# Two-layer transformer kernel on one core: float32 products of the FFNs, the router and the second Q, K, V written as three float16 products each

## The chip, the core and the metric

The kernel runs on one core of a Trainium2 chip. A core has a matrix engine (PE, its weight loads are shown apart as PEld), a vector engine (DVE), a scalar engine (ACT), GpSimd (POOL) and a queue engine (SP) that here starts every DMA. The engines run on their own and wait for each other by semaphores. Matrix products land in PSUM, eight banks of 512 float32 columns for each of 128 partitions; POOL doesn't work on PSUM in this kernel. The metric is the time of one execution in device microseconds, and the figure of a kernel is the median of its runs. Lower is better.

## What is computed

```python
x = L0_attn_x                                   # (1, 2048, 256), float32
h = _layernorm(x) * (1 + ca) + sa               # shifts and scales from silu(c) @ wmod
x = x + ga * _L0_attn_ref(h, ...)               # 16 heads of 16, causal with a distance penalty
h = _layernorm(x) * (1 + cb) + sb
x = x + gb * _L0_ffn_ref(h, ...)                # silu(h @ gate.T * s) * (h @ up.T * s) @ down.T * s, 704 wide
h = _layernorm(x) * (1 + ca) + sa               # layer 1, with its own shifts, scales and gates
x = x + ga * _L1_attn_ref(h, ...)               # 16 heads of 16, every query sees every key
h = _layernorm(x) * (1 + cb) + sb
scores = sigmoid(h @ gate_w.T)                  # router: 8 experts, the best 2 of each token are used
x = x + gb * (shared_out + routed_out)          # experts of 176 and a shared part of 352: 1760 wide
```

## The kernel before

The 2048 tokens are worked on in four chunks of 512 (`tc` or `p` from 0 to 3). One Python list, the walk, holds all work in program order; each engine runs through it and takes its own share of each item, so the list sets the order on every engine. It has five stages:

0. Prologue: modulation, first layer norm, Q, K, V of layer 0.
1. Attention of layer 0. Each score block is made twice: once for the row maxima (`max` items, PE L722 and the DVE reduction L1156), and once transposed for the exponentials (PE L753, ACT L951), followed by the product with V (PE L778).
2. FFN 0 in six pieces of its hidden width (`hg` = gate product L818, `hid` = up product L826, then silu on ACT L990 and the product with it on DVE L1180), with the tail of attention 0 between its first pieces, and from the second token chunk on the down product `dn` (L847) of the chunk before, its add to x (DVE L1147), statistics `st`, normalisation `nm` (DVE L1099), transposition `ln` (PE L684, evicted by ACT L927 into hT), and `qk`, `v` (L695, L707) of layer 1. K and V parts go to DRAM and come back into the layout of attention (SP L506, L533, L521; `keys` and `rows` items). Early `max` blocks of attention 1 are strewn in.
3. Attention of layer 1.
4. Router and FFN 1 in 14 pieces, of which eleven are routed and have their hidden values multiplied by the token's weight of the expert (PE `we` L835, ACT L1000, DVE L1184 and L1187), and three are shared. The first six gate and up pairs go with the tail of attention 1.

Weights, features hT and hidden values are float32 in the products that the change touches. POOL has little to do: the reciprocal root of the variance (L609, L612) for each `st`, the scaling of w_o and x's bias (L618, L625) and the scaling of the down weights (L635), also in the walk's order. The products of stage 2 and 4 use four slots of two PSUM banks; `hg` with its `hid` alternates between two of them, and waits until what was there two uses ago is drained.

## Time and profile before

| | |
|---|---|
| median of 3 runs | 1790.18 us (1787.64 to 1791.87) |
| profiled execution, its own time | 1790.27 us |
| its span in the trace | 1788.5 us |
| mean granted TensorE clock | 0.952 |
| busy: PE, PEld | 1649.3 us, 698.8 us |
| busy: DVE, ACT, POOL | 1166.7, 1004.2, 61.7 us |

The span is the time from the first to the last instruction in the trace. Busy times of engines overlap, so they don't add up to it. The share of an engine over the whole span hides the stages: what a change in a stage is worth has to be read from that stage's own windows.

### The profile page before, as it was taken

What the parts mean: (1) busy time and instruction counts of PE and PEld (TensorE: products, weight loads), DVE (VectorE), ACT (ScalarE), POOL (GpSimd) and SP (SyncE); (2) the same over time, 40 slices, a digit from 0 to 9 for tenths busy, and PEclk for the clock granted to TensorE, in tenths of its full rate; (3) what the DMA queues carried; (4) which work ended last, traced back from release to release, by engine and by line L of the source; (5) the groups of instructions that cost most, each with busy time, mean ns of one, the idle gap of its engine ahead of it and who ended that gap; (6) DMA issues with size and microseconds to landing.
All of it is one profiled execution on the core that took longest, in us unless ns stands there. A gap on an engine that the chain in (4) does not pass through costs nothing.

```text
span 1788.5 us, 32558 instructions
## 1 busy us (share of the span) xinstructions
PE 1649.3 (92%) x12812; PEld 698.8 (39%) x12812; DVE 1166.7 (65%) x1438; ACT 1004.2 (56%) x1913; POOL 61.7 (3%) x96
## 2 busy tenths in 40 slices
PE   7878988898999999859999999999999999999998
PEld 5533333333324544412333323333232244646556
DVE  5567888988912256694798999899989414231221
ACT  2145667777884111008997988789878952121120
POOL 2100000001000000300000000000000020000000
PEclk8879999999999999868999999999999989999999
DMA  7610000000001210110200000000000010000000
GB/s 212 148 50 11 11 11 6 11 6 1 2 1 30 46 45 20 34 40 6 87 6 6 6 6 6 6 6 9 8 2 2 1 42 1 6 6 12 1 12 12
DMA packets 39542, 41.87 MB, mean 23 GB/s; under 512 B 7172, under 2 KB 37828, under 8 KB 39388
## 3 DMA queue, kind: packets, MB, share of 16 engines
q1 hardware_dynamic: 39396, 39.79, 8.5%
q8 instruction: 108, 1.77, 0.4%
q14 instruction: 38, 0.31, 0.1%
HBM read 29.02 MB, written 10.49 MB: 22 GB/s over the span
## 4 chain that ended last, share of the span: by engine, by line
PE 61%; DVE 26%; ACT 6%; issue 3%; SPq 2%; DMA 2%; DVEq 0%; ACTq 0%
DVE mpart L1156 22%; PE psum L778 14%; PE psum L753 9%; PE psum L847 8%; PE psum L818 8%; PE psum L826 7%; PE psum L722 6%; ACT probs L951 5%; PE psum L695 2%; PE psum L807 1%; PE psum L684 1%; DMA parts<-key_region 1%; DVE attn_region L1099 1%; PE psum L761 1%; PE psum L835 1%
## 5 line engine op out<-in xcount | busy, mean ns | idle before, releaser
L1156 DVE TENSOR_REDUCE mpart<-psum 128x2 f32<-128x1024 f32 (+2 forms) x832 | 915.8, 1158 | 116.6 <-PE psum L722 92.4
L951 ACT ACTIVATE probs<-psum 128x512 f32<-128x512 f32 (+3 forms) x1664 | 844.4, 573 | 192.7 <-PE psum L753 108.0
L778 PE MATMUL psum<-probs,v_region 128*17 128x256 f32 (+2 forms) x6144 | 497.6, 396 | 13.8 <-ACT out_sb L966 9.9
L722 PE MATMUL psum<-key_region,row_region 50*128 50x512 f16 (+3 forms) x1664 | 327.1, 385 | 75.2 <-DVE mpart L1156 72.9
L753 PE MATMUL psum<-row_region,key_region 52*128 52x512 f16 (+3 forms) x1664 | 356.9, 381 | 13.8 <-ACT probs L951 8.2
L753 PEld LDWEIGHTS psum<-row_region,key_region 52*128 52x128 f16 x1664 | 98.8, 93 | 372.8 <-ACT probs L951 279.2
L778 PEld LDWEIGHTS psum<-probs,v_region 128*17 128x17 f32 x6144 | 103.0, 95 | 208.0 <-issue 103.4
L722 PEld LDWEIGHTS psum<-key_region,row_region 50*128 50x128 f16 x1664 | 94.3, 94 | 182.6 <-DVE mpart L1156 128.6
L818 PE MATMUL psum<-hT,ffn_w 128*128 128x512 f32 (+1 forms) x320 | 157.4, 615 | 1.7 <-issue 0.9
L826 PE MATMUL psum<-hT,ffn_w 128*128 128x512 f32 (+1 forms) x320 | 153.2, 602 | 0.0
L990 ACT ACTIVATE probs<-psum 128x512 f32<-128x512 f32 (+1 forms) x56 | 33.4, 597 | 190.2 <-PE psum L818 190.2
L1184 DVE TENSOR_TENSOR probs<-psum,probs 128x512 f32<-128x512 f32 x44 | 30.4, 691 | 106.5 <-PE psum L826 106.5
L847 PE MATMUL psum<-v_region,key_region 128*128 128x256 f32 x448 | 97.5, 379 | 1.7 <-DVE key_region L1187 1.7
L1147 DVE TENSOR_TENSOR x_sb<-psum,x_sb 128x512 f32<-128x512 f32 x16 | 11.1, 692 | 127.0 <-PE psum L847 127.0
L847 PEld LDWEIGHTS psum<-v_region,key_region 128*128 128x128 f32 x448 | 85.0, 190 | 15.4 <-issue 3.9
L826 PEld LDWEIGHTS psum<-hT,ffn_w 128*128 128x128 f32 (+1 forms) x320 | 59.6, 189 | 77.2 <-issue 77.2
L818 PEld LDWEIGHTS psum<-hT,ffn_w 128*128 128x128 f32 (+1 forms) x320 | 56.1, 187 | 69.4 <-issue 66.4
L990 ACT ACTIVATE probs<-psum,gate_s 128x512 f32<-128x512 f32 (+1 forms) x24 | 16.5, 687 | 102.1 <-PE psum L818 102.1
L927 ACT ACTIVATE hT<-psum,modc 128x512 f32<-128x512 f32 x32 | 23.2, 775 | 78.4 <-PE psum L684 78.4
L1180 DVE SCALAR_TENSOR_TENSOR key_region<-psum,up_s,probs 128x512 f32<-128x512 f32 (+1 forms) x24 | 18.0, 749 | 65.7 <-PE psum L826 65.5
L1190 DVE TENSOR_TENSOR key_region<-psum,probs 128x512 f32<-128x512 f32 (+1 forms) x12 | 8.2, 690 | 67.8 <-PE psum L826 67.6
L958 ACT ACTIVATE mrow_t<-psum 128x512 f16<-128x512 f32 x32 | 19.1, 598 | 51.6 <-PE psum L735 51.0
(102 smaller groups left out, 930.1 us busy)
## 6 DMA issues: line engine op xcount, KB each, us to landing
parts<-key_region SPq DMA_DIRECT2D x32, 256.0 KB, 2.5
key_region<-parts SPq DMA_DIRECT2D x48, 128.0 KB, 4.3
row_region<-parts SPq DMA_DIRECT2D x192, 32.0 KB
key_region<-in_wmod SPq DMA_DIRECT2D x2, 1536.0 KB, 12.1
x_sb<-in_x SPq DMA_DIRECT2D x4, 512.0 KB, 8.3
row_region<-mrow_t SPq DMA_DIRECT2D x128, 2.0 KB
out<-x_sb SPq DMA_DIRECT2D x16, 128.0 KB, 1.8
ffn_w<-in_w_gate SPq DMA_DIRECT2D x1, 1760.0 KB, 7.2
```

The lines of the kernel that those rows point to most:

```text
L695: mm = pe.matmul(bank(b + f), w[:, k, f * P:(f + 1) * P], hT[:, k, tc * CH:(tc + 1) * CH], start=(k == 0), stop=(k == KD - 1))
L722: mm = pe.matmul(bank(b + par)[:, 0:w], rows[at, g, hp, r * P:(r + 1) * P], keys[at, g * HP + hp, q * CH:q * CH + w], start=True, stop=not ...
L753: mm = pe.matmul(bank((e + par) % 3)[:, off:CH], keys[at, g * HP + hp, jt * P:(jt + 1) * P], rows[at, g, hp, off:CH], start=True, stop=not ...
L778: mm = pe.matmul(psum[32 * h:32 * h + VW, SUM_BANK, lo:hi], v_sb[:, jt, g * HG + h, :], probs[:, (S0[y] + s) % 2, h, lo:hi], start=(jt == ...
L818: mm = pe.matmul(psum[0:f, b, :], up_gate[y][0][:, d, c * P:c * P + f], hT[:, d, tc * CH:(tc + 1) * CH], start=(d == 0), stop=(d == KD - 1))
L826: mm = pe.matmul(psum[0:f, b + 1, :], up_gate[y][1][:, d, c * P:c * P + f], hT[:, d, tc * CH:(tc + 1) * CH], start=(d == 0), stop=(d == KD ...
L847: mm = pe.matmul(bank(b)[:, r * D:(r + 1) * D], hid[y][tc % 2][0:f, c, (2 * z + r) * P:(2 * z + r + 1) * P], down[y][0:f, c, :], start=(c ...
L927: ins = nc.scalar.activation(hT[:, c, tc * CH:(tc + 1) * CH], bank(b + c), ACT.Identity, bias=modc[:, y, i:i + 1], scale=modc[:, y, i + 2: ...
L951: nc.scalar.activation(probs[:, (S0[y] + s) % 2, 2 * hp + par, off:CH], psum[:, e % 3, off:CH], ACT.Exp, scale=SCALES[y]).then_inc(s_p, 1)
L990: nc.scalar.activation(sil[k % 2][0:f, :], psum[0:f, bank_of(item), :], ACT.Silu, scale=gate_s[0:f, c:c + 1] if y == 0 else 1.0).then_inc( ...
L1156: V.tensor_reduce(mpart[:, n % NG, at:at + 2, q:q + 1], psum[:, b:b + 2, 0:w], AX.X, ALU.max).then_inc(drained(*item)[0], 1)
L1184: V.tensor_tensor(utmp[k % 2], up, sil[k % 2], ALU.mult).then_inc(s_ut, 1)
```

## The change

Each float32 operand of the products in question is held as two float16 numbers, high = float16(a) and low = float16(a - high), in the room of the float32 word. A product is then the sum of three float16 products in PSUM: high by high, high by low, low by high (`PRODUCTS`). This is done for gate, up and down of both FFNs, the router's logits, and Q, K, V of layer 1. Attention 0's Q, K, V, the output projections and attention itself stay as they are.

The halves are made on the chip. Weights arrive in float32 in the key region and POOL splits them (`split_projections`, `split_ffn`, `split_down`). A transposed and modulated feature block is written twice by ACT, in float32 to a temporary and in float16 to hT, and POOL subtracts (`low_features`). Hidden values go to a float32 temporary, ACT makes the high half (`high_hidden`), and the low one is subtracted on POOL in layer 0 and on DVE in layer 1 (`low_hidden`, item `hh`, one pair late). In FFN 0 the down products move from behind the first to behind the second pair, `nm`, `ln`, `qk` and `v` move later; in FFN 1 the down products move by one pair too.

```diff
+PRODUCTS = ((0, 0), (0, 1), (1, 0))
...
-            if c == 0:
+            if c == 1:
                 for it in down_halves(0, p):
                     out.append(it)
                     blocks(2 * many if tc > 2 else 0)
                 out.append(("st", 2, p))
-            if c == 1:
+            if c == 3:
                 out.append(("nm", 2, p))
-            if c == 2:
+            if c == 4:
                 out.append(("ln", 2, p))
                 blocks(many)
-            if c == 4:
+            if c == 5:
                 out.append(("qk", 1, p, 0))
                 blocks(many)
                 out.extend([("qk", 1, p, 1), ("keys", 1, p)])
                 blocks(many)
                 if p == 0:
                     out.extend([("rows", 1, n) for n in range(NG)])
-            if c == 5:
                 out.append(("v", 1, p))
...
-    out += flat(second[:1]) + down_halves(1, 0) + flat(second[1:])
+    out += flat(second[:2]) + down_halves(1, 0) + flat(second[2:])
...
+    out += [("load", 0), ("wp",), ("wf", 0), ("wd", 0)]
...
+def with_halves(items):
+
+    out, open_one = [], None
+    for it in items:
+        if it[0] == "dn" and it[3] == 0 and open_one and open_one[1:3] == it[1:3]:
+            out.append(("hh", *open_one[1:]))
+            open_one = None
+        out.append(it)
+        if it[0] == "hid":
+            if open_one:
+                out.append(("hh", *open_one[1:]))
+            open_one = it
+    return out
...
+            def split_ffn(y):
+                pool.wait_ge(s_wffn[y], 32)
...
+                for d in range(KD):
+                    for i in range(2):
+                        link(nc.gpsimd.tensor_copy(up_gate[y][i][:, 0, d, :], raw_up_gate[y][i][:, d, :]))
+                        ins = nc.gpsimd.tensor_tensor(up_gate[y][i][:, 1, d, :], raw_up_gate[y][i][:, d, :],
+                                                      up_gate[y][i][:, 0, d, :], ALU.subtract)
...
                 for c in range(NC[y]):
                     f = fsize(y, c)
-                    ins = nc.gpsimd.tensor_tensor(down[y][0:f, c, :], down[y][0:f, c, :], gab[0:f, y, D:2 * D], ALU.mult)
+                    link(nc.gpsimd.tensor_tensor(down_t[0:f, c % 2, :], raw_down[y][0:f, c, :], gab[0:f, y, D:2 * D], ALU.mult))
+                    link(nc.gpsimd.tensor_copy(down[y][c][0:f, 0, :], down_t[0:f, c % 2, :]))
+                    ins = nc.gpsimd.tensor_tensor(down[y][c][0:f, 1, :], down_t[0:f, c % 2, :], down[y][c][0:f, 0, :], ALU.subtract)
...
+            def low_features(item):
+                q, tc = item[1:]
+                pool.wait_ge(*drained(*item))
+                for c in range(KD):
+                    ins = nc.gpsimd.tensor_tensor(hT16[tc][:, 1, c, :], mod_t[xh_buf(q, tc)][:, c, :], hT16[tc][:, 0, c, :], ALU.subtract)
+                ins.then_inc(s_low, 1)
...
-                for d in range(KD):
-                    mm = pe.matmul(psum[0:f, b, :], up_gate[y][0][:, d, c * P:c * P + f], hT[:, d, tc * CH:(tc + 1) * CH],
-                                   start=(d == 0), stop=(d == KD - 1))
+                pe.wait_ge(s_f16, y + 1)
+                pe.wait_ge(*split_of(2 * y + 1, tc))
+                for m, (u, v) in enumerate(PRODUCTS):
+                    for d in range(KD):
+                        mm = pe.matmul(psum[0:f, b, :], up_gate[y][0][:, u, d, c * P:c * P + f], hT16[tc][:, v, d, :],
+                                       start=(m + d == 0), stop=(m + d == len(PRODUCTS) + KD - 2))
...
                 pe.wait_ge(s_wd, y + 1)
-                for it in [it for it in walk if it[0:3] == ("hid", y, tc)][-2:]:
-                    pe.wait_ge(*drained(*it))
+                pe.wait_ge(s_lo, max(nth[it] for it in walk if it[0:3] == ("hh", y, tc)))
...
+                    for dst in (mod_t[xh_buf(q, tc)], hT16[tc][:, 0, :, :]):
+                        for c in range(KD):
+                            i = 4 * (q % 2) + c
+                            ins = nc.scalar.activation(dst[:, c, :], bank(b + c), ACT.Identity,
+                                                       bias=modc[:, y, i:i + 1], scale=modc[:, y, i + 2:i + 3])
...
+                nc.scalar.activation(hid[y][tc % 2][0:f, c, 0, :], utmp[k % 2][0:f, :], ACT.Identity).then_inc(s_hi, 1)
...
+            def low_hidden(item):
+                y, tc, c = item[1:]
+                k, f = nth[item], fsize(y, c)
+                dve.wait_ge(s_hi, k)
+                V.tensor_tensor(hid[y][tc % 2][0:f, c, 1, :], utmp[k % 2][0:f, :], hid[y][tc % 2][0:f, c, 0, :],
+                                ALU.subtract).then_inc(s_lo, 1)
```

Three places show how rows move. The first is PE in FFN 0, between the transposition for `ln` of token chunk 0 (L684 before, L788 in the change) and the first early `max` block of attention 1 (L722, L845). Before, with the transposition and one pair standing ahead of the first row:

```order
L818 MATMUL psum<-hT,ffn_w 128x512 x2
L826 MATMUL psum<-hT,ffn_w 128x512 x2
L695 MATMUL psum<-hT,w_row 128x512 x4
L695 MATMUL psum<-hT,w_col 128x512 x4
L818 MATMUL psum<-hT,ffn_w 64x512 x2
L826 MATMUL psum<-hT,ffn_w 64x512 x2
L707 MATMUL psum<-w_v,hT 128x256 x8
L818 MATMUL psum<-hT,ffn_w 128x512 x2
L826 MATMUL psum<-hT,ffn_w 128x512 x2
L847 MATMUL psum<-row_region,key_region 128x256 x24
L818 MATMUL psum<-hT,ffn_w 128x512 x2
L722 MATMUL psum<-key_region,row_region 128x512 x2
```

In the change, from that transposition to the same block (L942 and L951 are gate and up, L809 Q and K, L830 V; the down product, L973, comes three rows further):

```order
L788 MATMUL psum<-ident,attn_region 128x128 x8
L942 MATMUL psum<-hT,ffn_w 64x512 x6
L951 MATMUL psum<-hT,ffn_w 64x512 x6
L809 MATMUL psum<-hT,w_row 128x512 x12
L809 MATMUL psum<-hT,w_col 128x512 x12
L830 MATMUL psum<-w_v,hT 128x256 x24
L942 MATMUL psum<-hT,ffn_w 128x512 x6
L951 MATMUL psum<-hT,ffn_w 128x512 x6
L942 MATMUL psum<-hT,ffn_w 128x512 x6
L845 MATMUL psum<-key_region,row_region 128x512 x2
```

Q and K now stand behind one pair instead of two, V directly behind them, and the down product stands behind the first `max` block instead of ahead of it.

The second place is the end of POOL's program, which is the tail of attention 1 and the start of FFN 1. Before, the root for the chunk ahead, the scaling of the down weights and then the root for the last token chunk:

```order
L609 TENSOR_SCALAR vare<-mv 128x4
L612 TENSOR_TENSOR rstd<-vare,half 128x4
L635 TENSOR_TENSOR v_region<-v_region,gab 128x256 x13
L635 TENSOR_TENSOR v_region<-v_region,gab 96x256
L609 TENSOR_SCALAR vare<-mv 128x4
L612 TENSOR_TENSOR rstd<-vare,half 128x4
```

In the change the same place ends so (L713, L714, L715 make one piece of the down weights, and there are 14 such triples):

```order
L713 TENSOR_TENSOR key_region<-v_region,gab 96x256
L714 CAST v_region<-key_region 96x256
L715 TENSOR_TENSOR v_region<-key_region,v_region 96x256
L663 TENSOR_SCALAR vare<-mv 128x4
L666 TENSOR_TENSOR rstd<-vare,half 128x4
L724 TENSOR_TENSOR hT<-attn_region,hT 128x512 x2
```

The last reciprocal root (L663, L666) stands behind 42 instructions that wait for the down weights, where it stood behind 14, and the low half of the last features (L724) follows it.

The third place is SP's queue between the last `keys` of attention 0 (L533, L583) and the first placing of row maxima (L539, L589). Before:

```order
L533 DMA key_region<-parts 16x8x512 x6
L495 DMA ffn_w<-in_w_gate 128x2x704
L495 DMA ffn_w<-in_w_up 128x2x704
L499 DMA row_region<-in_w_down 128x5x256
L500 DMA row_region<-in_w_down 64x256
L539 DMA row_region<-mrow_t 2x512 x8
```

In the change:

```order
L583 DMA key_region<-parts 16x8x512 x6
L549 DMA row_region<-in_w_down 128x5x256
L550 DMA row_region<-in_w_down 64x256
L541 DMA key_region<-in_w_row 128x2x256
L541 DMA key_region<-in_w_col 128x2x256
L541 DMA key_region<-in_w_v 128x2x256
L545 DMA key_region<-in_w_gate 128x2x704
L545 DMA key_region<-in_w_up 128x2x704
L589 DMA row_region<-mrow_t 2x512 x8
```

Three loads, the projections of layer 1, now stand ahead of the first placing; the down weights come first and the FFN weights last.

## Rows read from the trace of the kernel before

**Rows 1.** The page, busy time and share of the span:

```profile
PE 1649.3 (92%) x12812; PEld 698.8 (39%) x12812; DVE 1166.7 (65%) x1438; ACT 1004.2 (56%) x1913; POOL 61.7 (3%) x96
```

**Rows 2.** Windows: PE, PEld, DVE, ACT, POOL busy (instructions), PE clock, DMA, GB/s:

```profile
575.50:620.00 44.50, 44.46 (x139) 24.05 (x138) 11.82 (x25) 9.55 (x14) 1.27 (x2) 1.00 0.09 29
670.70:723.70 53.00, 52.83 (x179) 24.76 (x177) 35.74 (x46) 8.10 (x12) 1.27 (x2) 1.00 0.17 37
723.70:766.00 42.30, 33.73 (x122) 18.40 (x120) 27.71 (x35) 3.98 (x6) 14.47 (x21) 0.80 0.15 34
1494.30:1788.50 294.20, 288.70 (x921) 163.76 (x919) 76.23 (x122) 56.83 (x79) 0.00 (x0) 1.00 0.02 8
```

**Rows 3.** FFN 1, timeline (start, duration, engine): two gates, an up's weights:

```profile
1633.68 1.88 PE L818 MATMUL psum<-hT,ffn_w 128*128 128x512 f32 x4
1635.39 1.88 PE L826 MATMUL psum<-hT,ffn_w 128*128 128x512 f32 x4
1635.40 0.19 PEld L826 LDWEIGHTS psum<-hT,ffn_w 128*128 128x128 f32 x1 [0.24 <-issue]
```

**Rows 4.** FFN 1: DVE's add behind a second down half, idle before it:

```profile
1633.88 0.69 DVE L1147 TENSOR_TENSOR x_sb<-psum,x_sb 128x512 f32<-128x512 f32 x1 [11.40 <-PE psum L847]
```

**Rows 5.** Timeline, 16-bit products: two of 512 columns, four of 128:

```profile
1512.23 0.60 PE L835 MATMUL psum<-row_region,esel 24*128 24x512 bf16 x2
1405.47 0.40 PE L735 MATMUL psum<-identh,mp 128*128 128x128 f16 x4
```

**Rows 6.** By form (busy, mean ns, idle): POOL's two, ACT's, DVE's:

```profile
L625 POOL TENSOR_TENSOR x_sb<-x_sb,b_o 128x256 f32<-128x256 f32 x32 | 22.2, 732 | 0.3 <-DVE attn_region L1099 0.2
L609 POOL TENSOR_SCALAR vare<-mv 128x4 f32<-128x4 f32 x16 | 3.7, 229 | 1261.0 <-DVE mv L1085 1258.3 <-issue 2.7
L927 ACT ACTIVATE hT<-psum,modc 128x512 f32<-128x512 f32 x32 | 23.2, 775 | 78.4 <-PE psum L684 78.4
L1187 DVE TENSOR_TENSOR key_region<-probs 128x512 f32<-128x512 f32 x44 | 30.4, 692 | 1.5
```

**Rows 7.** SP and PE where attention 0 starts:

```profile
84.00 0.43 SPq L495 DMA_DIRECT2D ffn_w<-in_w_gate  x1
95.29 0.61 PE L753 MATMUL psum<-row_region,key_region 52*128 52x512 f16 x2 [5.25 <-DMA row_region<-mrow_t]
```

**Rows 8.** FFN 0: K of token chunk 0, its way back, a down product:

```profile
609.26 3.60 PE L695 MATMUL psum<-hT,w_col 128*128 128x512 f32 x8
618.00 2.69 SPq L533 DMA_DIRECT2D key_region<-parts  x6
623.60 1.42 SPq L521 DMA_DIRECT2D row_region<-parts  x3
623.36 11.89 PE L847 MATMUL psum<-row_region,key_region 128*128 128x256 f32 x48
```

**Rows 9.** The page's DMA issues, KB and us to landing:

```profile
key_region<-parts SPq DMA_DIRECT2D x48, 128.0 KB, 4.3
```

**Rows 10.** DVE's normalisation, alone and beside POOL:

```profile
641.29 1.37 DVE L1099 TENSOR_SCALAR attn_region<-x_sb,mv,rstd 128x256 f32<-128x256 f32 x4
743.12 3.11 DVE L1099 TENSOR_SCALAR attn_region<-x_sb,mv,rstd 128x256 f32<-128x256 f32 x4
```

**Rows 11.** SP: keys of the last chunk, and the first placing of attention 1:

```profile
766.07 2.69 SPq L533 DMA_DIRECT2D key_region<-parts  x6
797.12 2.46 SPq L539 DMA_DIRECT2D row_region<-mrow_t  x4
```

**Rows 12.** Timeline, start of FFN 1:

```profile
1460.68 9.61 POOL L635 TENSOR_TENSOR v_region<-v_region,gab 128x256 f32<-128x256 f32 x14 [148.90 <-DMA v_region<-in_w_down]
1478.86 1.98 PE L818 MATMUL psum<-hT,ffn_w 128*128 128x512 f32 x4 [0.18 <-DVE key_region L1190]
1485.48 1.04 POOL L612 TENSOR_TENSOR rstd<-vare,half 128x4 f32<-128x4 f32 x1
1494.28 1.04 PE L684 MATMUL psum<-ident,attn_region 128*128 128x128 f32 x8
```

More of the change, by code:

```diff
@@ L267, in stages @@
     middle, done = ffn0_walk()
+    middle = with_halves(middle)
     return [prologue_walk(), attention_walk(0, []),
-            [("load", 1), ("wd", 0)] + middle + [("wo", 1)] + [("xb", 1, tc) for tc in range(NCH)],
-            attention_walk(1, done), [("load", 2), ("wd", 1)] + ffn1_walk()]
+            [("load", 1)] + middle + [("wo", 1)] + [("xb", 1, tc) for tc in range(NCH)],
+            [("load", 2), ("wf", 1)] + attention_walk(1, done), [("load", 3), ("wd", 1)] + with_halves(ffn1_walk())]
 IN_SLOT = ("mod", "ln", "qk", "v", "max", "mt", "ft", "bt", "op", "hg", "dn", "we", "lg", "rw")
@@ L474, in xh_buf, with split_of, routed_count @@
             return 1 if q % 2 else tc % 2
+        def split_of(q, tc):
+            return s_low, [it for it in walk if it[0] == "ln" and it[1]].index(("ln", q, tc)) + 1
+        def routed_count(tc, c):
+            return [it for it in walk if it[0] == "hid" and it[1] == 1 and it[3] < RC].index(("hid", 1, tc, c)) + 1
         def last_hid(tc):
@@ L578, in _ @@
                     place_maximum(*it[1:])
+                elif it == ("load", 0):
+                    load_down(0)
+                    sp.wait_ge(*filled("mod", 1))
+                    load_second_projections()
+                    load_ffn(0)
                 elif it == ("load", 1):
                     sp.wait_ge(*filled("op", 0, NCH - 1))
-                    load_attn(1)
+                    load_output(1)
                 elif it == ("load", 2):
+                    for b in range(2):
+                        sp.wait_ge(s_part[b], 16 * nth["qk", 1, NCH - 1, 1])
+                    sp.wait_ge(*filled("dn", 0, NCH - 1, 1))
+                    load_ffn(1)
+                elif it == ("load", 3):
                     sp.wait_ge(s_pv, S0[2])
                     load_down(1)
-                elif it[0] == "mp" and it[1:] == (1, 2):
-                    sp.wait_ge(s_mp, nth[it])
-                    load_ffn(1)
                 elif it[0] == "dn" and it[1] == 1:
@@ L1250, in _ @@
                     hidden(it)
+                elif it[0] == "hh" and it[1] == 1:
+                    low_hidden(it)
                 elif it[0] == "rt":
```

239 lines of the change are left out of this document (161 added, 78 removed).

## The prediction

> **What bounds the kernel now.** I read the page first: PE is busy for 92% of the span [rows 1]. That share is an average and proves little, so I cut the span by stage. The windows [rows 2] show PE without a gap in FFN 0's second and fourth token chunk (44.46 of 44.50 and 52.83 of 53.00 us) and almost so in FFN 1 (288.70 of 294.20), at full clock. DVE is busy there for 11.82, 35.74 and 76.23 us: room in FFN 1, little in FFN 0's last chunk. Only the tail of FFN 0 (33.73 of 42.30, clock 0.80) is a chain between engines. So in just the stages that the change touches, PE's own stream is the bound, and shorter products shorten the time until a chain is met.
>
> **Price of one product.** In FFN 1 a gate (two float32 products of 512 columns) starts at 1633.68 and the up behind it at 1635.39 [rows 3]: 1.71 us for two, 0.857 us each. The profile has four weight loads for them, each 0.19 us with 0.24 us of idle behind it: loading is covered by the products. A down half (28 products of 256 columns) has its add 0.69 + 11.40 = 12.09 us behind the other half's [rows 4], 0.432 each. The 16-bit price comes from products already there [rows 5]: two of 512 columns take 0.60 us with a modelled duration of about 0.38, so the second came 0.22 us later; I take 0.215 for 512 columns and half, 0.109, for 256. Does a 16-bit weight load hide behind 256 columns? Four loads with 128-column products take 0.40 us together, some 0.06 each once one duration of 0.22 is off, so a pair of load and product fits in 0.06 us, well under 0.109.
>
> A gate or up becomes six products, 1.29 us, and saves 0.42; a pair saves 0.84. A float32 product of 256 columns becomes 3 x 0.109 = 0.33 and saves 0.10; a down half of FFN 1 goes from 12.09 to 84 x 0.109 = 9.16 us and saves 2.9.
>
> **FFN 1.** Of its 56 pairs 50 lie in the window from 1494.30: 50 x 0.84 = 42.2 us. Eight down halves save 8 x 2.9 = 23. DVE's added low half is a block of about 0.69 us [rows 6], with two before makes 2.1 us a routed pair; ACT gets one block of at most 0.78. PE's new pair is 2.6 us and more with the spread weights, so both stay under it; the low half is made a pair late and PE doesn't wait for it. It does before the last down product, where high and low half stand in the chain: +1.5. I allow 2 more for slots.
>
> The first six pairs are another matter. Their 5 us and 2 of the logits (48 records of narrow products before, 72 products now, no dearer) run into two chains. PE already waits for DVE at 1478.86, behind the router's DVE work, and this wait grows by what PE gains before it. Then POOL: it scales the down weights from 1460.68 for 9.61 us (14 pieces), and only at 1485.48 makes the root for the last chunk, whose transposition starts at 1494.28 [rows 12]. In the change, each piece is scaled, cast and subtracted, with a wait behind each. Two two-input instructions of 256 cost 0.73 each [rows 6]; the cast lies between 0.23 (a one-input instruction of 4 elements) and 0.73. With 0.07 for each wait 14 pieces take 26 to 32 us, so POOL is free at 1485 to 1490 (loading starts up to 2 us earlier), the root and normalisation put the transposition at 1488 to 1493. I take 1491: of 7 us, 3 to 4 arrive. FFN 1 in sum: -42.2 - 23 - 3.7 + 3.5 = -65.
>
> The Trainium skill (GPSIMD Engine Reference, Elementwise side by side) has one-input work near 1.8 cycles an element at best and two-input work at 2.6; at its 1.2 GHz that is an estimate of some 0.4 us for the cast of 256, without its start. By it the 14 pieces would end near the middle of the range given.
>
> **FFN 0, saved.** 24 pairs x 0.86 = 20.5; four down products of 24 float32 products each, 72 x 0.109 = 7.9 us against the 11.8 that one takes now [rows 8]: 15.6; Q, K (8 x 0.84) 6.7; V (4 x 0.8) 3.2. Sum 46 us.
>
> **FFN 0, given back.** Four places, by what is late next.
> 1. *`ln` to `qk`, four times.* Before, two pairs of 3.4 us stood between. Now one of 2.6 does. The chain gets two more ACT blocks (0.73 each) and two POOL subtractions of 512. A POOL block of 256 is 0.73 us [rows 6], of which 0.23 at most is fixed, so 512 is 1.25 and the two 2.5. From the transposition's start the features are ready after 1.1 + 2.9 + 2.6 = 6.6 us; PE has 0.9 + 2.6 to do, and 1.5 more where three `max` blocks (0.5 each: two products as in [rows 5], partly side by side) stand between. Waits: 3.2, 1.7, 1.7, and in the tail, where nothing covered it before either, +2.4 after counting that x's bias is now behind it on POOL (below). 9 us.
> 2. *Keys and rows of attention 1.* K's products end at 612.8, the reload of keys is issued at 618.00, the first rows (four issues) until 625.0 [rows 8], and keys need 4.3 us to land [rows 9]: 12.2 us or more from K's end to the first `max`. Before, this lay under 24 us of V, two pairs and the down product. In the change the first `max` stands behind V (2.6), a pair and a gate (3.9), that is 6.5 us. PE waits 6 to 8 us, once. I take 7.
> 3. *Down products.* `dn` waits for the last low half on POOL. For chunk 0 this is queued behind the low features of the last chunk of attention 0: 2 us. For the last, it is DVE, ACT, POOL in a row, 2.2 us more than before. The pair now ahead covers the others.
> 4. *The tail of attention 0* (add, statistics, root, normalisation) was covered by three pairs of 3.4 us; three of 2.6 leave about 1 us open. In chunk 3 DVE has 37 us of work for about 44 of PE's: 2 us of waits.
>
> DVE beside POOL: its normalisation took 1.37 us alone and 3.11 beside POOL's bias work [rows 10]. POOL is now busy in FFN 0 for 12 us of each 45 and over the router's DVE work, which speaks against the change. In the tail it turns round: the bias work stands behind the low features, so that one slow normalisation (1.7 us) goes away, counted under 1. Elsewhere at most 3 normalisations could be hit, 5 us, and I charge none as likely, since few overlap. The Trainium skill (GPSIMD Engine Reference, Specifications) has the two contending for SBUF interfaces when DVE works in a 2-port mode or has two SBUF inputs. By that rule DVE's low halves in FFN 1, two SBUF inputs each, could be hit as well, but only while POOL splits the down weights, which is before 1490 and where DVE's router work is the chain already: the sum would be 3 us higher by it.
>
> PE's clock: in the tail, where PE idles, it is granted 0.80 on the mean [rows 2], that is partly the lower of its two levels. The 7 us wait will show the same; +2. In sum 9 + 7 + 4 + 3 + 2 = 25, so FFN 0 gives -46 + 25 = -21 us.
>
> **Attention.** The first scores wait 5.25 us until 95.29 for the placed maxima, which stand in SP's queue behind the weight loads that begin at 84.00 [rows 7]. These are 2112 KB in 11 us; the 768 KB added are 4 us more, on the path. The six `ln` of attention get 1.45 us of ACT each; ACT has gaps, I charge 3 in all. FFN 1's raw weights are loaded right behind the last keys, 3.5 MB or 18 us at the same rate; the next placing is issued at 797.12, 31 us after those keys (766.07) [rows 11], so it is hidden, as are POOL's splits during attention. Attention +7.
>
> **Sum.** -65 - 21 + 7 = -79 us on the span of 1788.5: 1709.5. The profiled execution took 1790.27, 1.8 more than its span, and the median is 1790.18, so the forecast is 1711 us.
>
> **Rivals.**
> - *The waits take more.* POOL's subtractions with mixed types could cost twice the 256-wide rows' rate: 2.5 us more at each `ln` (10), more at `dn` (5), POOL's 14 pieces near 50 us (the start of FFN 1 then 15 later), DVE beside it slower (5), clock at half for longer (5). Together up to 40: 1725 to 1755. For it: [rows 10] and the clock of the tail. Against it: POOL has 1.3 us to do in a pair of 3 to 3.6 and could take twice that. Four or five gaps of 2 to 7 us are in question for the clock. The Trainium skill (TensorE: Matmul & The Clock Gate, Why this matters for your kernels) warns that idle gaps between bursts of products bring the half clock back; the tail's 0.80 agrees.
> - *The waits overlap.* The long wait in chunk 2 lets the others catch up, and the first pairs of FFN 1 keep their gain: 1685 to 1692.
> - *Weight loads don't hide.* If a 16-bit load stood visibly between products, the 2208 new products would carry it. At 79 us / 2208 = 36 ns each the change gains nothing; with a load's 0.1 us beside each it would be near 1790 + 140 = 1930. [rows 5] speak against it, though with few products in a row; a long stream of 168 does not exist in this trace.
> - *PE is freed but another engine holds the pace in FFN 1.* DVE has 2.1 of 2.8 us a pair. If ACT's and DVE's new steps stood in the chain of the two slots, a pair would lose up to 0.8 us, and FFN 1's pairs their gain: 1755 to 1790. Against it: PE waits only for DVE's first product, which is no later than now.
>
> **How the numbers follow.** Forecast 0.62 (own range 1692 to 1727), waits take more 0.20, waits overlap 0.07, another engine 0.06, loads visible 0.05. The range must leave out 0.2: from 1692, above the overlap, to 1742, most of the waits. Within 0.2% (3.6 us, about what a measurement here can tell from no change) only edges of the last two lie: 0.02. Slower 0.04, faster 0.94.
>
> **What would show it.** Gates 1.29 us apart in FFN 1, and adds of down halves 9.2 apart; if they are 9.9 or more, the loads show. PE waiting 6 to 8 us for keys or rows ahead of the first early `max`; 2 to 3 us for POOL's L724 ahead of Q; the first scores of attention 0 at about 99 instead of 95.3; POOL's triples ending near 1488 less what is saved till then, and the last L788 behind it. Wrong would make it a PE clock under 0.9 in FFN 1 or POOL instructions of 512 over 2 us.

## The result, and the profile after

The changed kernel takes 1730.72 us (median of 4 runs, 1725.55 to 1732.33), the kernel before in the same measurement 1790.73 (4 runs): a ratio of 0.9664, 95% interval 0.9648 to 0.9679. That is 60 us less: inside the stated range of 1692 to 1742, but 19 us short of the 79 forecast. It is also above the forecast's own range (to 1727) and inside that of the rival "the waits take more" (1725 to 1755). The profiled execution took 1732.33 us, its span is 1730.3.

The busy line of the page, to be set beside [rows 1]:

```profile
PE 1533.4 (89%) x13548; PEld 637.8 (37%) x13548; DVE 1207.2 (70%) x1494; ACT 1061.6 (61%) x2017; POOL 177.8 (10%) x208
```

PE has 116 us less to do and the kernel is only 58 us shorter: half of what PE gained is lost again in its waits. The span cut at five landmarks (first scores of attention 0, first gate, first scores of attention 1, first logits, last `ln` transposition), after; the columns are the window and its length, PE, PEld, DVE, ACT and POOL busy with their instructions, the granted clock, DMA share and GB/s:

```profile
100.67:559.21 458.54, 406.96 (x4600) 156.48 (x4601) 340.46 (x415) 327.47 (x687) 32.56 (x43) 0.95 0.03 7
559.21:795.87 236.66, 183.03 (x1001) 88.98 (x1002) 152.68 (x197) 55.25 (x87) 78.81 (x71) 0.86 0.21 53
795.87:1450.24 654.37, 615.10 (x6074) 197.91 (x6070) 529.71 (x548) 566.99 (x1070) 10.61 (x12) 0.98 0.02 5
1450.24:1500.38 50.14, 29.95 (x188) 16.39 (x185) 24.21 (x45) 9.43 (x15) 30.90 (x44) 0.73 0.11 37
1500.38:1730.30 229.92, 221.37 (x1353) 127.81 (x1351) 107.70 (x174) 84.76 (x132) 2.27 (x2) 0.99 0.03 10
```

The same landmarks lie at 95.29, 548.94, 802.71, 1453.00 and 1494.28 us in the kernel before, which gives:

| stage | before | after | difference | predicted |
|---|---|---|---|---|
| to the first scores | 95.3 | 100.7 | +5.4 | +4 |
| attention 0 and 1 | 453.7 + 650.3 | 458.5 + 654.4 | +8.9 | +3 |
| FFN 0, start of attention 1 | 253.8 | 236.7 | -17.1 | -21 |
| FFN 1, start | 41.3 | 50.1 | +8.9 | -3.7 |
| FFN 1, rest | 294.2 | 229.9 | -64.3 | -61.7 |

The row of FFN 0 in the kernel before is

```profile
548.94:802.71 253.77, 226.31 (x744) 108.65 (x746) 148.41 (x197) 36.56 (x53) 19.54 (x29) 0.90 0.17 38
```

so PE is busy 43.3 us less in this stage (183.03 after) and idle 26.2 us more.

The long stages went as costed. PE's timeline in FFN 1, beside [rows 3]:

```profile
1510.91 1.46 PE L942 MATMUL psum<-hT,ffn_w 128*128 128x512 f16 x6
1511.99 1.18 PEld L951 LDWEIGHTS psum<-hT,ffn_w 128*128 128x128 f16 x6
1512.20 1.46 PE L951 MATMUL psum<-hT,ffn_w 128*128 128x512 f16 x6
```

A gate is followed by its up 1.29 us later, 0.215 us a product, and the loads lie under the products. The adds behind two down halves start 9.17 us apart (1551.79 and 1560.96), where 9.2 was forecast. What grew is the start of FFN 1, where PE is busy for 29.95 of 50.14 us at a clock of 0.73. The chain of waits there, from the timeline (start, duration, engine, in brackets the idle time and its releaser):

```profile
1459.11 1.52 POOL L713 TENSOR_TENSOR key_region<-v_region,gab 128x256 f32<-128x256 f32 x1 [140.57 <-DMA v_region<-in_w_down]
1478.99 0.38 DVE L1228 BATCH_NORM_AGGREGATE mv<-stats 128x2 f32<-128x6 f32 x4
1491.15 0.66 POOL L715 TENSOR_TENSOR v_region<-key_region,v_region 96x256 f16<-96x256 f32 x1
1492.10 1.04 POOL L666 TENSOR_TENSOR rstd<-vare,half 128x4 f32<-128x4 f32 x1
1493.17 1.38 DVE L1244 TENSOR_SCALAR attn_region<-x_sb,mv,rstd 128x256 f32<-128x256 f32 x4 [12.38 <-POOL rstd L666]
1494.47 2.04 DVE L1373 CAST row_region<-psum 24x512 bf16<-24x512 f32 x3
1495.19 0.60 PE L994 MATMUL psum<-identb,row_region 128*24 128x128 bf16 x4 [16.08 <-DVE row_region L1373]
1500.38 1.04 PE L788 MATMUL psum<-ident,attn_region 128*128 128x128 f32 x8
```

Read from the PE row L994 upward: PE waits 16.08 us for DVE's copy of the router's rows. That copy needs nothing of the normalisation, but stands behind it in DVE's order; the normalisation waits 12.38 us for POOL's root; and the root, whose statistics were ready at 1479.4, stands behind the 42 instructions of `split_down`. One late engine stopped the two others through their queues. Behind the copied rows PE still has one gate and one up ahead of the transposition, at a granted clock of 0.55 (1495.72 to 1500.38), close to the lower of its two levels. From the two instructions of the root (1491.79) to the transposition it takes 8.6 us.

A second place is the start of attention 1, where DVE writes the first maxima:

```profile
782.69 3.51 POOL L701 TENSOR_TENSOR ffn_w<-key_region,ffn_w 128x1760 f16<-128x1760 f32 x1
782.96 3.29 DVE L1315 TENSOR_SCALAR mp<-mx 128x16 f16<-128x16 f32 x1
786.14 1.65 POOL L700 CAST ffn_w<-key_region 128x1760 f16<-128x1760 f32 x1
786.29 1.58 DVE L1316 SCALAR_TENSOR_TENSOR mp<-mp,mx 128x16 f16<-128x16 f16 x1
789.01 0.61 PE L858 MATMUL psum<-identh,mp 128*128 128x128 f16 x4 [6.09 <-DVE mpart L1303]
```

DVE's two instructions on 16 columns end just as POOL's split of the FFN weights ends (786.25 against 786.20, 787.87 against 787.79); the median of the 32 L1315 is 203 ns. PE waits 6.09 us.

### The profile page after: what moved, and what is told of

It reads as the page before. It is cut to its first block, busy times and chain, and to the rows that moved or that the text cites. A ratio compares the mean times of both kernels' runs of the same rounds, so it can differ in the third digit from the quotient of the medians.

```text
span 1730.3 us, 34346 instructions
## 1 busy us (share of the span) xinstructions
PE 1533.4 (89%) x13548; PEld 637.8 (37%) x13548; DVE 1207.2 (70%) x1494; ACT 1061.6 (61%) x2017; POOL 177.8 (10%) x208
## 4 chain that ended last, share of the span: by engine, by line
PE 36%; DVE 18%; ACT 5%; issue 4%; POOL 3%; DMA 1%; SPq 0%; ACTq 0%; DVEq 0%; POOLq 0%
DVE mpart L1303 15%; PE psum L901 9%; PE psum L973 6%; PE psum L876 6%; PE psum L951 5%; PE psum L942 5%; PE psum L845 3%; ACT probs L1085 3%; PE psum L809 1%; POOL key_region L713 1%; PE psum L960 1%; POOL hT L724 1%; PE psum L930 1%; POOL v_region L715 1%; PE psum L788 1%
## 5 line engine op out<-in xcount | busy, mean ns | idle before, releaser
L1303 DVE TENSOR_REDUCE mpart<-psum 128x2 f32<-128x1024 f32 (+2 forms) x832 | 915.6, 1157 | 133.9 <-PE psum L845 105.0
L845 PE MATMUL psum<-key_region,row_region 50*128 50x512 f16 (+3 forms) x1664 | 326.1, 384 | 84.1 <-DVE mpart L1303 73.9
L845 PEld LDWEIGHTS psum<-key_region,row_region 50*128 50x128 f16 x1664 | 94.6, 94 | 181.3 <-DVE mpart L1303 130.8
L942 PE MATMUL psum<-hT,ffn_w 128*128 128x512 f16 (+2 forms) x480 | 121.2, 390 | 7.4 <-DVE probs L1329 6.2
L951 PE MATMUL psum<-hT,ffn_w 128*128 128x512 f16 (+2 forms) x480 | 120.6, 389 | 0.0
L1329 DVE TENSOR_TENSOR probs<-psum,probs 128x512 f32<-128x512 f32 (+1 forms) x56 | 38.7, 691 | 92.8 <-PE psum L951 87.2
L663 POOL TENSOR_SCALAR vare<-mv 128x4 f32<-128x4 f32 x16 | 3.6, 228 | 843.0 <-DVE mv L1228 840.3
L973 PE MATMUL psum<-v_region,key_region 128*128 128x256 f16 (+1 forms) x672 | 75.7, 276 | 3.0 <-DVE key_region L1340 3.0
L1294 DVE TENSOR_TENSOR x_sb<-psum,x_sb 128x512 f32<-128x512 f32 x16 | 11.1, 692 | 90.2 <-PE psum L973 90.2
L973 PEld LDWEIGHTS psum<-v_region,key_region 128*128 128x128 f16 (+1 forms) x672 | 66.4, 99 | 12.7 <-issue 3.5
L942 PEld LDWEIGHTS psum<-hT,ffn_w 128*128 128x128 f16 (+2 forms) x480 | 45.2, 102 | 67.8 <-issue 17.2
L951 PEld LDWEIGHTS psum<-hT,ffn_w 128*128 128x128 f16 (+2 forms) x480 | 48.1, 102 | 58.8 <-issue 7.8
L1132 ACT ACTIVATE key_region<-probs 128x512 f16<-128x512 f32 (+1 forms) x80 | 49.8, 622 | 15.2 <-DVE probs L1329 8.2
L1327 DVE SCALAR_TENSOR_TENSOR probs<-psum,up_s,probs 128x512 f32<-128x512 f32 (+1 forms) x24 | 17.9, 746 | 54.6 <-PE psum L951 44.1
## 6 DMA issues: line engine op xcount, KB each, us to landing
key_region<-in_wmod SPq DMA_DIRECT2D x2, 1536.0 KB, 11.6
```

Of the source, the lines that this page charges most:

```text
L845: mm = pe.matmul(bank(b + par)[:, 0:w], rows[at, g, hp, r * P:(r + 1) * P], keys[at, g * HP + hp, q * CH:q * CH + w], start=True, stop=not ...
L942: mm = pe.matmul(psum[0:f, b, :], up_gate[y][0][:, u, d, c * P:c * P + f], hT16[tc][:, v, d, :], start=(m + d == 0), stop=(m + d == len(PR ...
L951: mm = pe.matmul(psum[0:f, b + 1, :], up_gate[y][1][:, u, d, c * P:c * P + f], hT16[tc][:, v, d, :], start=(m + d == 0), stop=(m + d == le ...
L973: mm = pe.matmul(bank(b)[:, r * D:(r + 1) * D], hid[y][tc % 2][0:f, c, u, tok], down[y][c][0:f, v, :], start=(c + m == 0), stop=(c + m == ...
L1132: nc.scalar.activation(hid[y][tc % 2][0:f, c, 0, :], utmp[k % 2][0:f, :], ACT.Identity).then_inc(s_hi, 1)
L1303: V.tensor_reduce(mpart[:, n % NG, at:at + 2, q:q + 1], psum[:, b:b + 2, 0:w], AX.X, ALU.max).then_inc(drained(*item)[0], 1)
```

## The experiments

Each kernel was timed in turn with the kernel before; a ratio is compared with 0.9664 of the changed kernel, and a difference of 0.001 is 1.8 us. Line numbers shift by 1 to 8 where an edit adds lines.

**How far does PE hold the pace?** `e1_four` adds the product of the two low halves, `e2_two` leaves out the products of low weights with high activations, and their like elsewhere.

```
-PRODUCTS = ((0, 0), (0, 1), (1, 0))
+PRODUCTS = ((0, 0), (0, 1), (1, 0), (1, 1))      # e1_four
+PRODUCTS = ((0, 0), (0, 1))                      # e2_two
```

> The changed kernel with the fourth product of halves (low by low) added everywhere. If TensorE holds the pace of both FFNs and a 512-column float16 product costs its 0.215 us wherever it stands, this adds 320 products of 512 columns in gate and up (68.8 us), 320 of 256 columns in the down products (34.9), 32 and 32 in Q, K and V (10.4) and 32 short ones: 115 us on 1730.7, so 1846, or 3% slower than before the change. Rival, the waits of the FFN stages are overlapped by the longer products (a wait for GpSimd, for a transfer, for the router): then some 30 us of waits shrink, and it ends near 1815 to 1830.

> The changed kernel with one product of halves fewer (it leaves out low weights by high activations in gate and up, and its like elsewhere). If TensorE alone holds the pace, 115 us go: 1616. Rival, VectorE or ScalarE is next: a routed pair has three VectorE steps of 0.69 us = 2.07 against TensorE's 1.72 + 0.22, so each of the 44 routed pairs gives back at least 0.13 us, and waits that stand now (GpSimd, keys and rows) lose the products that cover them, 1 to 2 us at each of some ten places: 1630 to 1650, with TensorE waiting for VectorE inside the pairs of the second FFN.

Measured: 1829.71 us (ratio 1.0218, 1.0186 to 1.0249) and 1660.82 us (0.9266, 0.9239 to 0.9294), so +99 and -70 us where PE alone would give 115 each way. With four products it ends in the rival's range (1815 to 1830). By stage, from the same landmarks (full price: 67 in the rest of FFN 1, 41 in FFN 0, 5 at FFN 1's start):

| | FFN 0 | FFN 1, start | FFN 1, rest |
|---|---|---|---|
| fourth product added | +29.9 | +0.7 | +64.5 |
| third product removed | -15.7 | -3.5 | -54.8 |

In the rest of FFN 1 PE is the bound at three products and nearly so at two, where it waits 14.3 us for DVE (5.1 with three). FFN 0 is bound by PE for three quarters of a product more and for little over a third of one fewer; the start of FFN 1 hardly at all. Waits of PE in FFN 0 with four products, then with two (us in total, times, longest):

```profile
PE psum L809 <- POOL hT L724: 7.9, 4, 4.4
PE psum L845 <- DMA row_region<-parts: 5.2, 1, 5.2
PE psum L788 <- DVE attn_region L1244: 0.8, 1, 0.8
```

```profile
PE psum L845 <- DVE mpart L1303: 29.6, 46, 2.4
PE psum L788 <- DVE attn_region L1244: 11.0, 5, 3.7
PE psum L845 <- DMA row_region<-parts: 9.1, 1, 9.1
```

The same chains are more and more uncovered as PE's cover shrinks. The expected 1616 of a pure PE bound was wrong, and 1630 to 1650 still 11 too low.

**The down split ahead of the root.**

```
-            [..., [("load", 3), ("wd", 1)] + with_halves(ffn1_walk())]
+            [..., [("load", 3)] + with_halves(ffn1_walk())]
...
         if m == 4:
             out += [("rw", tc) for tc in range(NCH - 1)]
+    out.append(("wd", 1))
```

> The second layer's split of the down weights on GpSimd moves from the start of the stage to behind the last normalisation of that stage's start. Theory: the 33 us of 42 GpSimd instructions hold back the reciprocal root of the last token chunk, VectorE stands in order behind it, and the router's rows come 16 us late. Then the 16 us wait of TensorE for the router's rows goes, the router's steps on VectorE fall back to 0.96 us from 1.3, and the kernel takes 12 to 16 us less, 1715 to 1719; the first down half, which now needs the split later, still finds it done. Rival, the router itself or its steps in line on VectorE are late: then 0 to 4 us less. Second rival, the split now meets the first routed pairs' VectorE steps from SBUF, which it slows, and gives back 5 us or more.

Measured: 1719.76 us, ratio 0.9605 (0.9575 to 0.9636), 11 us less. The start of FFN 1 takes 30.8 us instead of 50.1, the rest 234.8 instead of 229.9. The root, the wait for the router's rows, and a new wait:

```profile
1476.26 1.04 POOL L667 TENSOR_TENSOR rstd<-vare,half 128x4 f32<-128x4 f32 x1
1479.35 0.60 PE L995 MATMUL psum<-identb,row_region 128*24 128x128 bf16 x4 [3.61 <-DVE row_region L1374]
1513.27 2.74 PE L943 MATMUL psum<-hT,ffn_w 128*128 128x512 f16 x6 [5.95 <-DVE probs L1330]
```

The theory holds: 16.08 became 3.61. Another 3.0 us come from PE's wait for DVE behind the router's first part (4.11 before the edit at 1470.55, 1.09 with it at 1469.84), and the products behind that wait run at a granted clock of 1.00 instead of 0.50. The second rival holds too, with 4.9 us, since the split now meets the routed pairs and the router's second part. How the two engines meet, in the same kernel:

```profile
1499.36 0.69 DVE L1335 TENSOR_TENSOR probs<-probs 128x512 f32<-128x512 f32 x1
1499.42 1.21 POOL L714 TENSOR_TENSOR key_region<-v_region,gab 128x256 f32<-128x256 f32 x1
1499.96 1.22 DVE L1341 TENSOR_TENSOR key_region<-probs,key_region 128x512 f16<-128x512 f32 x1
1500.69 0.74 POOL L715 CAST v_region<-key_region 128x256 f16<-128x256 f32 x1
```

L714 takes 0.73 alone, L1341 0.69, L715 0.40. These three are longer by 0.48, 0.53 and 0.34 us, where 0.63, 0.67 and 0.49 us were left of the other engine's instruction as they began: each waited for most of it, in turn. Not every DVE step on SBUF data does. In the changed kernel a reduction with one SBUF input and a POOL multiplication run side by side, neither longer than alone (0.25 and 0.72):

```profile
1465.73 0.72 POOL L713 TENSOR_TENSOR key_region<-v_region,gab 128x256 f32<-128x256 f32 x1
1465.80 0.25 DVE L1360 TENSOR_REDUCE row_region<-row_region 128x12 f32<-128x96 f32 x1
```

**The FFN 1 weight split behind the first maxima.**

```
                 if y:
                     pool.wait_ge(*filled("hid", 0, NCH - 1, NC[0] - 1))
+                    pool.wait_ge(s_mp, nth["mp", 1, 0])
```

> The second FFN's weights are split only after VectorE has written the first maxima of the second attention. Theory: VectorE's two small steps on SBUF data there (3.29 and 1.58 us where the median is 0.20 and 0.23) stand still while GpSimd's 3.5 and 1.65 us instructions run. With GpSimd idle there they take 0.2 us each, TensorE's wait of 6.1 us ahead of the transposed maxima falls to about 1.7, and the kernel takes 4.4 us less, 1726.3. But the splitting then meets other maxima of the attention, each of which has small VectorE steps on SBUF too; where they are covered nothing shows. Rival, the steps are slow for another reason (the first of the stage): no change.

Measured: 1726.54 us, ratio 0.9640 (0.9617 to 0.9664), 4.2 us less by the medians, but the interval overlaps the changed kernel's, so the time alone doesn't tell; the trace does:

```profile
780.00 0.20 DVE L1316 TENSOR_SCALAR mp<-mx 128x16 f16<-128x16 f32 x1
780.24 0.23 DVE L1317 SCALAR_TENSOR_TENSOR mp<-mp,mx 128x16 f16<-128x16 f16 x1
780.63 1.65 POOL L701 CAST ffn_w<-key_region 128x1760 f16<-128x1760 f32 x1 [29.40 <-DVE mp L1317]
781.61 0.61 PE L859 MATMUL psum<-identh,mp 128*128 128x128 f16 x4 [1.66 <-DVE mpart L1304]
```

With POOL idle the two take 0.20 and 0.23 us at the same place of the program, and PE's wait falls from 6.09 to 1.66. That they are slow as the first of their stage is out.

**Keys and rows under the down halves.**

```
-            out.append(("hg", 0, tc, c))
-            blocks(many if (tc, c) != (2, 0) else 0)
+            some = {(2, 0): 0, (2, 1): 0, (2, 2): 2 * many}.get((tc, c), many)
+            out.append(("hg", 0, tc, c))
+            blocks(some)
...
```

> In the third token chunk of the first FFN the maxima of the second attention that stood in pair (2,1) move into pair (2,2), behind the two down halves of some 17 us. Theory: TensorE's 7.2 us wait for the parts of keys and rows coming back from memory has nothing to cover it; behind the down halves it is covered, the wait goes, the half-clock stretch behind it too (some 2 us), and the kernel takes 7 to 9 us less, 1722 to 1724. Rival, VectorE becomes the pace: pair (2,2) then holds four reductions of maxima on one pair of banks and its own product, and gives back 2 to 4 us: 1725 to 1728.

Measured: 1727.97 us, ratio 0.9637 (0.9617 to 0.9657): by the median 2.8 us less, the interval overlaps the changed kernel's. In the changed kernel PE's rows read

```profile
624.52 1.46 PE L942 MATMUL psum<-hT,ffn_w 128*128 128x512 f16 x6
633.19 0.61 PE L845 MATMUL psum<-key_region,row_region 50*128 50x512 f16 x2 [7.21 <-DMA row_region<-parts]
633.74 2.72 PE L951 MATMUL psum<-hT,ffn_w 128*128 128x512 f16 x6
```

(the six products behind the wait take 2.64 us to the next instruction, at a granted clock of 0.52, near the lower of its two levels); with the edit this wait is gone, but new ones stand behind the down halves, such as:

```profile
641.06 0.39 PE L846 MATMUL psum<-key_region,row_region 50*128 50x512 f16 x2 [0.56 <-DVE mpart L1304]
650.27 1.06 PE L789 MATMUL psum<-ident,attn_region 128*128 128x128 f32 x8 [0.73 <-DVE attn_region L1245]
```

The stage is 5.2 us shorter in this profile. A wait of 7.2 us was worth less than itself: the median lies in the rival's range.

**Loads behind the first placing.** The item `("load", 0)` moves from the end of the prologue's order behind `("place", 0, 0)`.

> The loads of the first layer's down, FFN and the second layer's projection weights go behind the first placing of maxima in SyncE's order instead of ahead of it. Theory: they keep the queues busy while the first maxima are placed, 2.3 us of TensorE's wait, and they delay the loads that the start waits for: 2 to 5 us less, 1726 to 1729. Rival: the start of the kernel differs from run to run by as much with the same code (first scores at 96.6 to 102.1 us in four kernels with one start), the transfer is small, and nothing can be told: within 2 us of 1730.7. In the trace the wait of the first scores tells: 7.5 us falls to about 5.3, or stays.

Measured: 1724.73 us, ratio 0.9620 (0.9597 to 0.9643), 6 us less by the medians and the intervals don't overlap. SP now issues the placing before the loads:

```profile
84.91 2.49 SPq L589 DMA_DIRECT2D row_region<-mrow_t  x4
87.44 0.40 SPq L549 DMA_DIRECT2D row_region<-in_w_down  x1
90.22 0.61 PE L876 MATMUL psum<-row_region,key_region 52*128 52x512 f16 x2 [1.60 <-DMA row_region<-mrow_t]
```

The first scores start at 90.2 us; in the eight kernels with the old order (the changed one, e1 to e5, e7, e8) they start at 96.6 to 102.1, on the mean 99.6. PE's wait there fell from 7.5 to 1.6 us: the loads were four fifths of it, not the 2.3 us by which it had grown.

**ScalarE's added blocks.**

```
-                    for dst in (mod_t[xh_buf(q, tc)], hT16[tc][:, 0, :, :]):
+                    both_parts = (mod_t[xh_buf(q, tc)], hT16[tc][:, 0, :, :])
+                    for dst in both_parts[:1] if q % 2 and tc < NCH - 1 else both_parts:
...
+                if q % 2 and tc < NCH - 1:
+                    for c in range(KD):
+                        ins = nc.gpsimd.tensor_copy(hT16[tc][:, 0, c, :], mod_t[xh_buf(q, tc)][:, c, :])
+                    link(ins)
```

> For the normalised features of both attentions' feed-forward inputs (three of four token chunks each) ScalarE writes only the float32 copy; GpSimd makes the float16 high half as well as the low one. It takes 12 ScalarE blocks of about 0.6 us off a stream of exponentials that TensorE waits for in both attentions. Theory: these blocks are what the attentions lost (4.9 and 4.1 us by one profile): 5 to 8 us less, 1723 to 1726. Rival: the attentions' lengths differ from run to run by as much (455.7 to 463.1 us in the first, 654.4 to 657.8 in the second, over six profiles in which their code is the same), the blocks cost 3 us or less, and the kernel takes 0 to 3 us less, 1728 to 1731.

Measured: 1718.11 us, ratio 0.9583 (0.9565 to 0.9602), 12.6 us less by the medians, more than either theory gave. PE's wait for ScalarE's exponentials in the whole kernel, in the one before, the changed one, and this one:

```profile
PE psum L753 <- ACT probs L951: 8.2, 28, 0.9
```

```profile
PE psum L876 <- ACT probs L1085: 16.3, 32, 2.2
```

```profile
PE psum L880 <- ACT probs L1090: 8.7, 28, 0.9
```

Before and here 28 waits of at most 0.9 us, after 32 of up to 2.2. One of them, the two new ACT blocks between PE's transposition and the next exponentials, and PE's wait behind them:

```profile
183.51 1.45 ACT L1061 ACTIVATE attn_region<-psum,modc 128x512 f32<-128x512 f32 x2 [3.47 <-PE psum L788]
184.85 1.44 ACT L1061 ACTIVATE hT<-psum,modc 128x512 f16<-128x512 f32 x2
```

```profile
186.52 0.28 PE L876 MATMUL psum<-row_region,key_region 52*128 52x128 f16 x1 [2.16 <-ACT probs L1085]
```

Attention 0 takes 450.0 us here and attention 1 651.3, against means of 460.1 and 656.7 over the eight profiles of kernels that leave the attentions' code alone (455.7 to 463.1, 654.4 to 657.8). Against the changed kernel's own profile (458.5 and 654.4) the two are 11.6 us shorter, against the means 15.5, and in the kernel of all six edits below, whose attentions have the same code, 455.0 and 650.6, which is 11.2 under the means. The twelve blocks are 8.7 us of ACT's time and the waits named for ACT fell by 7.6 us. That the blocks cost the attentions some 8 us is shown; why the kernel gained more than that is not.

**Normalisation one pair earlier.**

```
-            if c == 3:
+            if c == 2:
                 out.append(("nm", 2, p))
-            if c == 4:
+            if c == 3:
                 out.append(("ln", 2, p))
```

> In the first FFN the normalisation moves from pair 3 to pair 2 and its transposes from pair 4 to pair 3, with the second layer's Q and K staying in pair 5, as far from the transposes as before the change. Theory: TensorE's waits for GpSimd's low halves ahead of Q and K (2.9, 1.5 and 1.2 us) and their half-clock stretches go: 4 to 6 us less, 1725 to 1727. Rival: VectorE's normalisation then stands sooner in line behind GpSimd's root, whose queue holds the low halves of the pairs before, VectorE stops for it and TensorE waits for VectorE instead: 0 to 3 us either way.

Measured: 1729.77 us, ratio 0.9648 (0.9629 to 0.9668): no difference that can be told. Waits of PE in FFN 0, the changed kernel, then this one:

```profile
PE psum L809 <- POOL hT L724: 10.1, 4, 4.4
PE psum L788 <- DVE attn_region L1244: 4.1, 3, 1.9
```

```profile
PE psum L788 <- DVE attn_region L1244: 7.4, 5, 2.1
PE psum L809 <- POOL hT L724: 4.4, 1, 4.4
```

The waits ahead of Q and K went except for the tail's (-5.7 us), and 3.3 us came back ahead of the transpositions. The rival had the size right and its mechanism only in part: DVE stops for POOL's root for 0.50 and 0.40 us in the first two chunks, but its second and third normalisation take 3.20 and 2.24 us instead of 1.54 and 1.37, since they now run beside POOL.

**All six edits together.**

> The six edits of the runs before together: down split late, FFN split late, maxima behind the down halves, loads behind the first placing, GpSimd makes the high halves, normalisation a pair earlier. If each mended a wait of its own, their differences to the 1730.7 of the changed kernel add up: 11 + 4.2 + 2.8 + 6 + 12.6 + 1 = 37.6 us, 1693. Rival, some share a wait or GpSimd's added casts of the high halves collide with VectorE's small steps in the attentions: a third is lost, 1700 to 1706. Either way below every kernel so far.

Measured: 1683.38 us (1682.86 to 1688.76), ratio 0.9417 (0.9396 to 0.9438): 106 us less than before the change, 47 less than the change alone. The six single ratios lie 0.0059, 0.0024, 0.0027, 0.0044, 0.0081 and 0.0016 under 0.9664; their sum 0.0251 gives 0.9413. So the measured ratio is what full adding up would give. This is weaker than it looks: the changed kernel's ratio enters the sum six times, and with the intervals given the sum is uncertain by about 0.011, some 19 us, so that a loss of a third isn't excluded. The total is firm, the sum of the parts is not. My 1693 came from medians against the changed kernel's, which was timed on another occasion. Attention 0 and 1 take 455.0 and 650.6 us, FFN 0 221.3, FFN 1 28.1 and 235.9.

## Why the prediction held, and where it was off

**Right.** *PE's own stream is the bound, and a product costs 0.215 us for 512 columns*: shown by the 1.29 us between gate and up, and by the fourth product, which adds 64.5 of 67 us in the rest of FFN 1. With it the rivals "weight loads don't hide" and "another engine holds the pace" are out. The rest of FFN 1 gave 64.3 us where 61.7 was predicted (50 pairs, eight down halves, 3.5 of ends and slots, most of which did not come). *FFN 0's gains less its four waits*: -17.1 for -21, and 4.6 of the difference is the maxima's wait at the start of attention 1 (1.50 us before, 6.09 after), which the stage as cut contains. PE is idle 26.2 us more; without that wait it is 21.6, where 25 was charged for waits and clock. The single waits were sized well: keys and rows 7.2 us (7 taken), `ln` to `qk` 2.92, 1.53, 1.22 and 4.42 us, 10.1 in sum with the tail's full wait, of which 0.7 stood there before (9 taken), `dn` of chunk 0 1.3 (2 taken). The last `dn` doesn't wait (2.2 taken). *Loads ahead of the first placing*: +4 taken; 99.6 on the mean against 95.3 (one profile) is +4.3, and with the loads moved most of the wait is gone. *POOL's prices*: 0.73 for the multiplication, 0.67 for the subtraction, 0.40 for the cast of 256 columns (0.4 was the estimate, without its start), and 1.16 for a subtraction of 512.

**Off.** Three steps account for most of the shortfall. Undoing them shows the first in time and trace, the second in time (not all of its size is explained), and the third in the trace. A fourth is smaller and was not undone.
1. *The start of FFN 1: "the root and normalisation put the transposition at 1488 to 1493. I take 1491: of 7 us, 3 to 4 arrive."* The split ran for 32.7 us (1459.1 to 1491.8) where 26 to 32 was allowed, because its first instructions and the router's on DVE blocked each other, and the transposition came at 1500.38. The sum allowed 3 us from POOL being free (1485 to 1490) to the transposition (1488 to 1493). Its own [rows 12] have the root at 1485.48 and the transposition at 1494.28, 8.8 us apart, and after the change it is 8.6. It followed the root and the normalisation and did not ask what stands behind them: in DVE's order the router's rows, which PE needs for a product ahead of the transposition, and on PE the gate and up at the low clock. This is the largest term, 12.6 us from the forecast: 5.6 from this step, most of the rest from POOL being free later. Moving the split gives back 19.3 there (17.3 to 17.7 against five other kernels with the changed order, whose stage takes 48.1 to 48.5) and 11 net.
2. *"ACT has gaps, I charge 3 in all."* The blocks fall between a transposition and the exponentials that PE waits for, so the gaps elsewhere don't cover them. On the mean of eight profiles the attentions take 12.8 us more than in the one profile of the kernel before, 10 over the charge; without the blocks 12.6 us of time go. What goes beyond the blocks' own 8.7 us stays open.
3. *"Elsewhere at most 3 normalisations could be hit, 5 us, and I charge none."* I looked for DVE beside POOL only at the normalisations and the router. *"As are POOL's splits during attention"* was taken as hidden because no one waits for their result, though DVE's two small steps at 782.96 stood beside them on the path: 4.4 us. Two normalisations were hit as well, 3.05 and 2.28 us where 1.37 is the price alone, with waits of PE of 1.95 and 1.37 us behind them. The Trainium skill (GPSIMD Engine Reference, Specifications) has the engines contend when DVE has two SBUF inputs or works in a 2-port mode; the trace agrees for L1316, which has two SBUF inputs and was slowed, and for the reductions from PSUM and from one SBUF input, which were not. L1315 was slowed with one SBUF input; in what mode it ran no row shows. The trace adds the size: one small step stands still for nearly the whole of a 3.5 us instruction.
4. *"72 x 0.109 = 7.9 us against the 11.8 that one takes now [rows 8]: 15.6."* The 11.8 is FFN 0's own row, the 0.109 is FFN 1's price. In FFN 0 the 72 products take 8.69 us (636.71 to the next gate at 645.40), 0.121 each, so a down product saves 3.1 instead of 3.9 and the four 12.5 instead of 15.6. With that the 46 us to be saved become 43, and PE's busy time in the stage fell by 43.3.

By the table the misses are 1.4, 5.9, 3.9 and 12.6 us less the 2.6 that FFN 1's rest gave beyond its charge: 21 us, the whole of what the span lacks. By the steps, 12.6 + 10 + 4.4 - 2.6 = 24 us; the 3 us between the two are less than the 7 by which one attention differs between profiles of the same code, and FFN 0's smaller gain and smaller waits cancel. So the direction and PE's price were understood, and the total was not: the measured time lies in the band of the rival "the waits take more", and that the stated range still holds it, with two chains not seen, is partly luck. That rival had the size of the start of FFN 1 nearly right (15 us) but for a price of POOL near 50 us, which was not it: POOL's price was as forecast, the queue behind it was not seen.

## What to carry to other kernels

When work is added to a helper engine, look not only for who waits for its result but for every instruction queued behind it, and for what is queued behind those on the next engine; then for small steps of its neighbour that lie on the path while a long instruction runs. Gaps cover added work only where they lie between the same two events. A wait's length is a guess at what removing it gives: 7.2 us of wait were worth some 3 to 5, and another edit gave more than the waits it took away. Where single edits are small, compare each with the kernel before in its own runs, and don't trust a sum of their differences to better than their intervals allow. When a chain is priced, read its length from the rows of the kernel before, from end to end, and not only the steps that come to mind.

## What the runs showed of the hardware

- GpSimd and some VectorE instructions stop each other for most of a whole instruction, in both directions: a step of 0.20 us took 3.29 beside a 3.51 us subtraction of GpSimd, and GpSimd's 0.73 and 0.40 became 1.21 and 0.74 beside VectorE. The VectorE instructions seen in this are those with two SBUF inputs, scalings (TENSOR_SCALAR) and casts from SBUF to SBUF (L1365, 0.56 us instead of 0.21). Reductions and products that read PSUM kept their time (L1303 2.34 for two, L1329 0.69) beside the same GpSimd instructions, and so did a reduction from SBUF with one input (L1360, 0.25).
- Float16 weight loads of 128 columns (98 to 102 ns) stay hidden behind 256-column products in streams of 168, two down halves of FFN 1 in 18.35 us, 0.109 us a product. In FFN 0, where every sixth piece is only 64 wide, 72 such products took 8.69 us, 0.121 each; why was not looked into.
- In eight kernels that leave the attentions' code alone the first attention takes 455.7 to 463.1 us, a spread of 7 us, while 230 us of the second FFN repeat to within 0.1 us in six of the kernels.
